# Edge network of a graph kernel: waits on signals in place of emptying VectorE's pipe, and three product tiles in place of two

## The reference, cut to what matters

```
w = relu(edgefeats @ fnet_w1 + fnet_b1) @ fnet_w2 + fnet_b2
W = w.reshape(-1, nc, nc)
for _ in range(NREPEATS):                  # 2
    xj = hx[edge_src]
    m = jnp.einsum('ei,eio->eo', xj, W)
    agg = segment_sum(m, edge_dst) * inv_deg[:, None]
    hx = _gru_cell(agg, hx, gru_w_ih, gru_w_hh, gru_b_ih, gru_b_hh)
```

## Time and profile before

| what | us |
|---|---|
| median of three runs | 22240.44 (22239.56 to 22242.14) |
| the profiled execution, span from its first to its last instruction | 30666.4 |
| VectorE busy in it | 18344.5 |
| TensorE busy in it | 19689.1 |
| GpSimd busy in it | 16237.0 |

### The profile page before, as it was taken

One profiled execution on the slowest core, in us unless ns is written; L12 is line 12 of the kernel. 1 busy time (PEld: TensorE's weight loads), 2 busy tenths in 40 slices (PEclk: granted clock), 3 DMA queues, 4 the chain that ended last, 5 costly groups with the idle time before them and its releaser, 6 DMA issues.

```text
span 30666.4 us, 276253 instructions
## 1 busy us (share of the span) xinstructions
PE 19689.1 (64%) x89726; PEld 9475.3 (31%) x89726; DVE 18344.5 (60%) x38447; ACT 2899.0 (9%) x6609; POOL 16237.0 (53%) x16846
## 2 busy tenths in 40 slices
PE   4466657767567776455555477777566665777775
PEld 1122223333223333233333233333333333333332
DVE  6566657777567777456666465555455554555554
ACT  3344400000000000100000000000000000000000
POOL 5555555555455555445555555555355554454555
PEclk8788878888778888677777688888688886888887
DMA  3333322222122222133333122222233332222221
GB/s 122 83 103 104 101 52 66 68 66 66 45 62 68 66 68 67 32 85 88 85 86 91 45 77 76 76 76 76 62 93 93 93 91 66 55 55 55 56 56 44
DMA packets 1271680, 2237.21 MB, mean 73 GB/s; under 512 B 386665, under 2 KB 737274, under 8 KB 1261818
## 3 DMA queue, kind: packets, MB, share of 16 engines
q1 hardware_dynamic: 729380, 2025.85, 19.9%
q0 software_dynamic: 538944, 192.26, 6.7%
q10 hardware_dynamic: 1942, 1.43, 0.0%
HBM read 1597.46 MB, written 620.66 MB: 72 GB/s over the span
## 4 chain that ended last, share of the span: by engine, by line
DVE 36%; another core or an unknown queue 27%; PE 22%; DVEq 7%; issue 7%; POOL 1%; DMA 0%; ACT 0%; ACTq 0%; SPq 0%; POOLq 0%
PE psB L768 17%; DVE Sb L1284 6%; DVE xT L1164 5%; DVE prod L1325 5%; DVE xT L1160 4%; DVE sub L1170 4%; DVEq L1169 3%; PE psB L839 2%; DVE prod L1328 1%; DVEq L1193 1%; DVE arena L1131 1%; DVEq L1324 1%; PE psB L905 1%; PE psA L799 1%
## 5 line engine op out<-in xcount | busy, mean ns | idle before, releaser
L768 PE MATMUL psB<-xp,arena 128*128 128x476 bf16 x26040 | 6949.8, 421 | 3618.6 <-DVE xT L1164 2521.8
L768 PEld LDWEIGHTS psB<-xp,arena 128*128 128x128 bf16 x26040 | 2630.0, 108 | 7599.1 <-issue 5550.5
L768 PE MATMUL psB<-ext,arena 128*128 128x308 bf16 (+1 forms) x17388 | 3670.7, 366 | 1826.4 <-issue 1114.7
L1160 DVE TENSOR_TENSOR xT<-psB,XT 128x616 bf16<-128x616 f32 (+1 forms) x1860 | 1803.2, 977 | 3128.9 <-remote 2508.0
L532 POOL DMA_INDIRECT gb<-tab3b,typi x2356 | 2269.1, 963 | 2348.7 <-DVE xT L1160 1489.5
L532 POOL DMA_INDIRECT gb<-tab1b,srci x2356 | 2293.3, 973 | 1929.0 <-issue 645.4
L532 POOL DMA_INDIRECT gb<-tab1a,srci x2356 | 2297.1, 975 | 1905.3 <-issue 651.3
L532 POOL DMA_INDIRECT gb<-tab2a,srci x2232 | 2111.8, 946 | 2047.6 <-DVE xT L1160 1350.0
L532 POOL DMA_INDIRECT gb<-tab2b,srci x2356 | 2229.3, 946 | 1789.9 <-DVE xT L1160 1043.6
L1164 DVE TENSOR_TENSOR xT<-psB,sub 128x476 bf16<-128x476 f32 x2976 | 1920.1, 646 | 2039.8 <-remote 1670.1
L532 POOL DMA_INDIRECT gb<-tab3a,typi x2108 | 2093.8, 993 | 1897.2 <-DVE xT L1164 1015.9
(11 more groups left out here) (337 smaller groups left out, 19385.5 us busy)
## 6 DMA issues: line engine op xcount, KB each, us to landing
arena<-oh_d SPq DMA_DIRECT2D x1861, 448.0 KB
hid<-oh_d SPq DMA_DIRECT2D x639, 448.0 KB
oh_d<-arena SPq DMA_DIRECT2D x558, 448.0 KB
ext<-oh_d SPq DMA_DIRECT2D x290, 448.0 KB
S2a<-Sb SPq DMA_DIRECT2D x62, 1404.0 KB
S2b<-Sb SPq DMA_DIRECT2D x62, 884.0 KB
ext<-in_attrT SPq DMA_DIRECT2D x404, 128.0 KB
S3a<-Sb SPq DMA_DIRECT2D x62, 832.0 KB
```

Of the source, the lines that this page charges most:

```text
L768: m = pe.matmul(psB[b][:, o:o + W], pk.onehot(n)[:, g, u * P:(u + 1) * P], pk.part(g, q).bitcast(BF16), start=g == 0, stop=g == NB - 1)
L1160: v.tensor_tensor(to.rearrange("p (b f x) -> p b f x", b=2, x=2 * JB), psB[b][:, :].rearrange("p (b w) -> p b w", b=2)[:, :, 0:W].rearrang ...
```

## The change

In `net_pass`, and nowhere else:

- the drain ahead of each group's product and the one ahead of the last sum go away;
- each sum (but the last of a chunk, which signals `d_gbfree` as before) now signals `d_message`, a new semaphore;
- from the fourth group of a chunk on, a product waits for `d_message` of the sum three groups back, the last reader of its tile;
- each sum waits for `d_product` of its own product;
- products go to three tiles in turn, the third being a free piece of `arena`.

The drain at the start of a chunk, the one ahead of the scans and those of the picks stay.

```
@@ -1310,24 +1310,27 @@
             def net_pass(rep):
...
-                pr = [prod[:, i * 1024:(i + 1) * 1024].rearrange("p (t o i) -> p t o i", t=4, o=16) for i in range(2)]
+                groups = TC // 4
+                pr = [t.rearrange("p (t o i) -> p t o i", t=4, o=16) for t in (prod[:, 0:1024], prod[:, 1024:2048], arena[:, 2816:3840])]
...
                         done = picks(k, done, pk.until(c, 0.9 * i * 4 / TC), 16)
                         v.wait_ge(t_weight, NG * rep + g + 1)
-                        v.drain()
-                        m = v.tensor_tensor(pr[i % 2], psB[g % 2][:, :].rearrange("p (t o i) -> p t o i", t=4, o=16),
+                        if i >= 3:
+                            v.wait_ge(d_message, (NCH * rep + c) * (groups - 1) + i - 2)
+                        m = v.tensor_tensor(pr[i % 3], psB[g % 2][:, :].rearrange("p (t o i) -> p t o i", t=4, o=16),
                                             bc(gv[:, 4 * i:4 * i + 4, :], 2, 16), ALU.mult).then_inc(d_product, 1)
                         if i:
-                            v.tensor_reduce(msg[:, 4 * i - 4:4 * i, :], pr[(i - 1) % 2], AX.X, ALU.add)
-                    v.drain()
-                    v.tensor_reduce(msg[:, TC - 4:TC, :], pr[(TC // 4 - 1) % 2], AX.X, ALU.add).then_inc(d_gbfree, 1)
+                            v.wait_ge(d_product, NG * rep + g)
+                            v.tensor_reduce(msg[:, 4 * i - 4:4 * i, :], pr[(i - 1) % 3], AX.X, ALU.add).then_inc(d_message, 1)
+                    v.wait_ge(d_product, NG * rep + (c + 1) * groups)
+                    v.tensor_reduce(msg[:, TC - 4:TC, :], pr[(groups - 1) % 3], AX.X, ALU.add).then_inc(d_gbfree, 1)
```

More of the change, by code:

```diff
@@ L254, in gnn_program @@
             sem(f"d_{n}") for n in ("first", "zero", "key16", "find", "count", "cum", "ends"))
-        d_code, d_keep, d_row, d_typed, d_gbfree, d_sum, d_product, d_xe, d_zz = (
-            sem(f"d_{n}") for n in ("code", "keep", "row", "typed", "gbfree", "sum", "product", "xe", "zz"))
+        d_code, d_keep, d_row, d_typed, d_gbfree, d_sum, d_product, d_message, d_xe, d_zz = (
+            sem(f"d_{n}") for n in ("code", "keep", "row", "typed", "gbfree", "sum", "product", "message", "xe", "zz"))
         d_fix, d_fixexp, d_fixrow, d_input, d_evac, d_mid, d_act, d_block, d_stage, d_nodes = (
@@ L1319, in net_pass @@
                     v.drain()
-                    for i in range(TC // 4):
-                        g = c * TC // 4 + i
+                    for i in range(groups):
+                        g = c * groups + i
                         done = picks(k, done, pk.until(c, 0.9 * i * 4 / TC), 16)
                         v.wait_ge(t_weight, NG * rep + g + 1)
-                        v.drain()
-                        m = v.tensor_tensor(pr[i % 2], psB[g % 2][:, :].rearrange("p (t o i) -> p t o i", t=4, o=16),
+                        if i >= 3:
+                            v.wait_ge(d_message, (NCH * rep + c) * (groups - 1) + i - 2)
+                        m = v.tensor_tensor(pr[i % 3], psB[g % 2][:, :].rearrange("p (t o i) -> p t o i", t=4, o=16),
                                             bc(gv[:, 4 * i:4 * i + 4, :], 2, 16), ALU.mult).then_inc(d_product, 1)
                         if i:
-                            v.tensor_reduce(msg[:, 4 * i - 4:4 * i, :], pr[(i - 1) % 2], AX.X, ALU.add)
-                    v.drain()
-                    v.tensor_reduce(msg[:, TC - 4:TC, :], pr[(TC // 4 - 1) % 2], AX.X, ALU.add).then_inc(d_gbfree, 1)
+                            v.wait_ge(d_product, NG * rep + g)
+                            v.tensor_reduce(msg[:, 4 * i - 4:4 * i, :], pr[(i - 1) % 3], AX.X, ALU.add).then_inc(d_message, 1)
+                    v.wait_ge(d_product, NG * rep + (c + 1) * groups)
+                    v.tensor_reduce(msg[:, TC - 4:TC, :], pr[(groups - 1) % 3], AX.X, ALU.add).then_inc(d_gbfree, 1)
                     done = sums(k, c, 16, done, range(16), lambda q: msg[:, :, q], lambda q: same[:, span(c)])
```

## The result

The changed kernel takes **21958.35 us** (median of four, 21951.42 to 21971.21); the kernel before, beside it, 22241.29 us (22239.56 to 22251.71). The ratio is 0.9873 with a 95% interval of 0.9861 to 0.9885: 283 us faster, 256 to 309 by the interval. The forecast was 22000 us, in a range of 21945 to 22170.

A forecast was written before the change was run, and what follows sets the result against it. The prediction took VectorE to bound the net passes; dropped drains would save 1.91 us a chunk, 237 us over two passes of 62 chunks, so 22240 - 237 = 22003, said as 22000 us, range 21945 to 22170.

The forecast's parts named there:

- these waits: Waits of unknown releaser in the profiled chain, 8280 us: taken to come with profiling and left out of every stretch.
- VectorE sets the pace of the net passes: Net passes: VectorE takes 51.8 us a chunk without remote waits, 50.5 without the others too, while GpSimd waits for it.
- with its 48.8, which just fits: Net passes, after the change: GpSimd's gathers need 48.8 us a chunk, next to VectorE's 48.6 to 49.9.
- The price of a drain: Ahead of products: each drain removed saves 0.17 us behind a pick and 0.15 behind a pair's sum.
- the saving of VectorE: Both net passes: drains removed ahead of products and the last sum save 1.91 us a chunk, 237 us in all.
- I cost these two (0.07 and 0.17) at nothing: TensorE hides them: First two products of a chunk: late TensorE weights swallow their drain saving; without that cover 0.24 us a chunk more.
- The new waits at nothing: Sums and products waiting for VectorE's own signals: always met, cost taken as nothing; other bound 0.17 us each.
- The free drain: Products reading PSUM after another engine's signal start only with the pipe empty, so nothing is saved: 22240 us; chance 5%.
- The wait that empties the pipe: Sums and ten products a chunk: waiting for VectorE's own signal empties the pipe, 211 us slower, 22451 us; chance 5%.
- TensorE staying late: Second half of a chunk's products: they wait for TensorE too, half the saving is lost, 22120 us; chance 4%.
- GpSimd taking over: Net passes: GpSimd's chunk of 49.5 or 50.3 us limits the gain to 124 or 25 us; chance 24%.
- the prediction's own sign: Profile after: VectorE's first product of a chunk waits for gathers; GpSimd's idle time behind line 1333 nearly vanishes.

## Why the prediction was right, and where it was off

**The stretched profile.** "I take these waits to come with the profiling" was wrong. They come with the kind of chip: 30495 us without a profile. Leaving them out was still what the forecast needed, since the chip that was timed doesn't have them, and that was luck; the agreement of 8280 and 8426 us was that between two kinds of chip. Nor is their releaser outside of the kernel: they are VectorE's waits for TensorE, so the 44.6 us that the prediction gave as TensorE's whole part in line 1325's waits lacked the 619.2 beside it.

**Who paces.** "VectorE sets the pace of the net passes" holds on the chips where the kernel before was profiled; on the timed kind it is inferred. For the changed kernel GpSimd "with its 48.8, which just fits" is right: 48.8 us a chunk, and 20 us of waits of GpSimd in 2800.

**The price of a drain.** 0.17 behind a pick and 0.15 behind a pair's sum; before, 0.09 and 0.07 after the end; after, 0.09 and 0.08 before it: 0.18 and 0.15. Right, and with the drains put back the gain was gone.

**The term that was mis-sized** is the saving of VectorE, 1.91 us a chunk, 237 us, against 2.36 in the starts of the two profiles (50.26 less 47.90). Of the 0.45 between them 0.24 is "I cost these two (0.07 and 0.17) at nothing: TensorE hides them". That rested on one turn, where the second product stood idle for 1.23 us. Over all 122 turns of the same profile it started within 0.15 us of the end ahead of it in 63 and idled over 0.5 us in 39; in the profile after it started before that end in 77. So TensorE hides the second drain at some turns and not at most. Another 0.13 was in no term: a sum now starts 1.13 us after the product ahead of it in place of 1.14 (4500.75 to 4501.88, against 6508.81 to 6509.95 in the earlier trace rows), 12 times a chunk, and the product's mean time is 1216 ns in place of 1225. The rest is rounding.

**How much of it arrived.** The timed kernel gained 283 / 124 = 2.28 us a chunk. That is near VectorE's own 2.36, but the two can't simply be set equal: after the change VectorE waits 0.9 us a chunk for gathers and weights, and what it waited before on such a chip wasn't profiled. So how the 283 us split over these terms stays open.

**The new waits at nothing.** Right: sums that wait for VectorE's own signal start before the product's end. Where such a signal is waited for at once it costs 0.19 us, so it is the distance of two groups, or the pick between, that makes them free.

**The rivals.** The free drain is refuted by the starts. The Trainium skill, "VectorE: DVE Perf Modes", section "The DRAIN you can't avoid", has the next operation wait until the pipe is empty, and adds that one that isn't held starts earlier; the prediction left the addition out, and it is the addition that the starts here bear out. The wait that empties the pipe is refuted by the same rows. TensorE staying late took nothing from the gain on the chips of the experiments, where its late signals are 14 us a chunk; on the timed kind it left 36 us of waits in both passes. GpSimd taking over came true in mechanism, by the prediction's own sign: first products wait for gathers, 91 us over both passes, and its idle time behind line 1333 is 0.3 us in 2800. The loss that it foretold, a gain of 124 or 25 us in place of 237, did not show: GpSimd's chunk stayed at 48.8 us and not 49.5 or 50.3, and the inferred 51.1 us of the kernel before lie above the 50.5 that this rival started from. That the forecast came within 42 us owes something to terms that pulled against each other.

## What to carry to other kernels

An explicit drain between two large independent VectorE operations cost some 0.16 us here, read as the difference between "starts after the end" and "starts before the end" of the one ahead, and not from the DRAIN's own duration. A signal and a wait on the same engine in its place were free with a pick of half a microsecond between. When the profiled span and the timed runs differ by a third, run the kernel again before explaining it, and when a wait has no releaser in the profile, look up which semaphore the program waits for there. Before taking one turn between chunks as the rule, count the others. And before moving an operation out of the way of a critical one, look at whom it may give time.

## What the runs showed of the hardware that was not expected

The same kernel takes 22.24 ms on one chip and 30.13, 30.20 and 30.50 ms in three series on chips of the other kind, without a profile. The changed kernel's mean granted clock is 0.807 there and 0.908 on the chip that was timed, and VectorE of the kernel before waits some 14 us in each chunk for signals of TensorE that come late after the recorded end of its matmuls, 11.3 us in the case shown above. The transfers of the hardware queue aren't slower there: its packets take 18.7% of 3800 us for 232.2 MB in the profile ahead of the prediction, and 25.5% of 2800 us for 232.6 MB in the one after, 3.1 us a MB in both. On those chips two gathers of 38 less a chunk brought 200 us. What holds the signals back stays open.
